# Routed experts of the first layer for three rows on scattered token blocks, the last row dense; constants of the key operands set earlier

## The reference, cut to what matters

```python
h = layernorm(x) * (1 + ca) + sa                # layer 0
x = x + ga * causal_attention_16_heads(h)       # 8 numbers a head, plus a shared rotary part of 32
h = layernorm(x) * (1 + cb) + sb
shared = gelu(h @ sW1 + sb1) @ sW2 + sb2        # one shared expert, 512 wide
w = softmax(h @ gW + gb)                        # 15 routed experts
topv, topi = top_k(w, 3)
gated = sum_over_k(one_hot(topi) * topv)
routed = sum_over_e(gated[e] * (gelu(h @ rW1[e] + rb1[e]) @ rW2[e] + rb2[e]))   # each 256 wide
x = x + gb * (shared + routed + h)
h = layernorm(x) * (1 + ca) + sa                # layer 1
x = x + ga * (attention_16_heads(h, no mask) @ w_proj + b_proj)
h = layernorm(x) * (1 + cb) + sb
x = x + gb * top_1_of_8_experts(h)              # relu, each 512 wide
```

## Time and profile before

| | |
|---|---|
| three runs, median (lowest to highest) | 937.01 us (936.86 to 939.99) |
| profiled execution: own time / span in the trace | 944.65 us / 942.9 us |
| mean granted clock of TensorE | 0.936 |
| TensorE products (PE) / weight loads (PEld) | 781.0 us, 83% / 492.7 us, 52% |
| VectorE (DVE) | 651.1 us, 69% |
| ScalarE (ACT) | 533.4 us, 57% |
| GpSimd (POOL) | 245.3 us, 26% |
| moved by DMA | 46.84 MB |

### The profile page before, as it was taken

How to read it: one execution, slowest core, us unless ns; L and a number is a source line. 1 busy time by engine, 2 the same in 40 slices (tenths; PEclk the granted TensorE clock), 3 DMA queues, 4 the chain that set the end, 5 groups by cost and what they waited for, 6 DMA issues and landing times. The chain is left out here.

```text
span 942.9 us, 12902 instructions
## 1 busy us (share of the span) xinstructions
PE 781.0 (83%) x4212; PEld 492.7 (52%) x4212; DVE 651.1 (69%) x1292; ACT 533.4 (57%) x976; POOL 245.3 (26%) x323
## 2 busy tenths in 40 slices
PE   4798888889987999999989789989989998338750
PEld 2454545445554677778767534444444443227740
DVE  5475586776672876866767696788988884438843
ACT  1345445546556677777767456656656666126740
POOL 3237655524421100000000230012212231144425
PEclk9589899999999999999999999999999999759985
DMA  5323411111100770000001121221321310021013
GB/s 167 68 62 90 85 25 31 36 36 35 27 10 1 224 223 0 1 1 1 1 12 22 31 62 34 43 72 24 83 43 37 89 25 13 0 74 45 29 37 87
DMA packets 56671, 46.84 MB, mean 50 GB/s; under 512 B 5831, under 2 KB 46620, under 8 KB 56604
## 3 DMA queue, kind: packets, MB, share of 16 engines
q1 hardware_dynamic: 55435, 43.72, 19.4%
q0 software_dynamic: 1024, 2.10, 0.8%
q10 hardware_dynamic: 144, 0.20, 0.1%
HBM read 14.67 MB, written 14.55 MB: 31 GB/s over the span
## 5 line engine op out<-in xcount | busy, mean ns | idle before, releaser
L923 ACT ACTIVATE ring<-single 128x512 f32<-128x512 f32 (+3 forms) x512 | 253.1, 518 | 196.8 <-PE single L1188 189.2
L1577 DVE TENSOR_REDUCE mneg<-pair 128x2 f32<-128x1024 f32 (+3 forms) x256 | 258.3, 1022 | 71.2 <-PE pair L1172 31.9
L1188 PE MATMUL single<-q_op,k_op 128*128 128x512 f32 (+3 forms) x512 | 215.7, 440 | 14.3 <-ACT ring L923 9.1
L1168 PE MATMUL pair<-k_op,q_op 128*128 128x512 f32 (+3 forms) x512 | 167.6, 406 | 13.0 <-DVE mneg L1577 11.4
L1188 PEld LDWEIGHTS single<-q_op,k_op 122*128 122x128 f32 (+1 forms) x512 | 96.8, 195 | 95.7 <-ACT ring L923 74.0
L1168 PEld LDWEIGHTS pair<-k_op,q_op 120*128 120x128 f32 (+1 forms) x512 | 98.2, 203 | 54.0 <-DVE mneg L1577 34.7
L1205 PE MATMUL p_o<-ring,vaug 128*9 128x512 f32 (+3 forms) x1024 | 114.0, 517 | 1.0 <-ACT ring L923 0.9
L1629 DVE TENSOR_TENSOR ring<-ring,single 128x1024 f32<-128x1024 f32 x60 | 73.2, 1221 | 46.9 <-ACT ring L952 45.4
L952 ACT ACTIVATE ring<-pair,cols 128x512 f32<-128x512 f32 x136 | 86.2, 686 | 32.5 <-PE pair L1252 26.7
L1634 DVE TENSOR_TENSOR hid_lo<-ring,hid_hi 128x1024 fp32r<-128x1024 f32 x68 | 83.3, 1224 | 22.9 <-ACT hid_hi L967 19.5
L967 ACT ACTIVATE hid_hi<-ring 128x1024 fp32r<-128x1024 f32 x68 | 72.2, 1062 | 31.3 <-issue 30.5
(11 more groups left out here) (311 smaller groups left out, 1347.7 us busy)
## 6 DMA issues: line engine op xcount, KB each, us to landing
xs<-zero SPq DMA_DIRECT2D x10, 1024.0 KB, 10.2
k_op<-hl SPq DMA_DIRECT2D x112, 64.0 KB
q_op<-hl SPq DMA_DIRECT2D x16, 256.0 KB
stage<-in_L_ffn_W_dram SPq DMA_DIRECT2D x8, 512.0 KB, 5.0
stage<-in_L_ffn_rW_dram SPq DMA_DIRECT2D x6, 512.0 KB, 4.9
q_op<-hl SPq DMA_DIRECT2D x48, 64.0 KB
xb<-xs SPq DMA_DIRECT2D x15, 128.0 KB, 2.0
xs<-yb SPq DMA_DIRECT2D x15, 128.0 KB, 1.7
```

The costliest lines, as they stand in the source:

```text
L923: exp_done.by(act.activation(ring[:, n % 8, lo:T], singles[n % 2][:, lo:T], ACT.Exp), (L, n))
L1168: ins = pe.matmul(both[:, i, 0:hi], r32(qs[:, P * qt:P * (qt + 1)]), r32(ks[:, 0:hi]), start=i == 0 or L == 1 or qt >= 2, stop=L == 1)
L1188: st_full.by(pe.matmul(singles[n % 2][:, lo:T], r32(ks[:, P * kc:P * (kc + 1)]), r32(qs[:, lo:T]), start=True, stop=True), (L, n))
L1577: s_taken.by(dve.tensor_reduce(mneg[:, G % 2, 2 * p:2 * p + 2, qt], both[:, :, 0:hi], axis=AX.X, op=ALU.max, negate=True), (L, m))
```

## The change

The key operands' constants are set in two memsets: those of the first eight heads right after the memset of `w_qkv`, those of the last four after the small memsets.

The routed experts of rows 0 to 2 are no longer dense. For each of these rows three parts are added beside the quads of the next row: `ht` transposes the high part of h back to rows of tokens, `rk` ranks each token's three choices within their experts and makes slots, and `bt` (once, after row 2) makes the table of blocks. GpSimd scatters each row's tokens with 12 indirect DMAs into a store cut into 13 x 1 MB, which SyncE cleared in rows 0 and 1 with transfers from the zeroed `w_qkv`. Between the attention and the dense stage stands a new loop, `routed_rows`, over 32 blocks (`NBLK0`) of 256 slots; its number is fixed by the sizes, not by where tokens go. Beside it stand the parts of the last row's output, norm and router (`BESIDE0`). The dense stage has 23 units left: the two shared ones for rows 0 to 2, all 17 for row 3. GpSimd gathers the results with 12 indirect DMAs a row, and `add_experts` (parts `c0`, `c1`, `c2`) weights them and adds them on VectorE. Weights of the second layer's attention are scaled in place, where copies were made before, and loads for the second layer go out in row 2.

```diff
+SPARSE = NB - 1
...
+NBLK0 = (TOP * T * SPARSE + E0 * (BLK - 1)) // BLK
+STORE = E0 * CAP0 + NBLK0 - TOP * T * SPARSE // BLK
+SLOTS = 8
...
-          (8, "b"): ["T.hin"], (8, "d"): ["T.lg"], (9, "b"): ["ot1"], (9, "d"): ["T.ex"], (10, "b"): ["mt3"],
...
+          (8, "b"): ["T.hin"], (8, "d"): ["T.lg"], (9, "b"): ["ot1", "T.ht"], (9, "d"): ["T.ex"], (10, "b"): ["mt3"],
+          (10, "d"): ["T.rt1"], (11, "b"): ["T.rt2"], (12, "b"): ["T.gt"], (12, "d"): ["T.rk"], (13, "b"): ["ot2"], (14, "b"): ["P.mt0"]},
...
+UNIT = [(r, u) for r in range(SPARSE) for u in (E0, E0 + 1)] + [(NB - 1, u) for u in range(UNITS)]
...
-DSTEPS = NB * UNITS + DEPTH + 3
...
...
+BESIDE = {7: ["c0"], 8: ["tb0"], 9: ["P.ns"], 10: ["P.na", "tb1"], 11: ["P.n1", "P.n2"], 12: ["P.n3", "P.ne"], 13: ["P.ln1"], 14: ["tb2"],
+          15: ["P.q"], 16: ["tb3"], 17: ["P.k", "c1"], 18: ["wo1"], 19: ["P.v"], 22: ["c2"]}
...
+            def clear(n):
+                first = 8 * BLK * n
+                sp.dma_start(xs[first:first + 8 * BLK, :].rearrange("(p b) d -> p b d", p=P),
+                             w_qkv[:, 0:D].unsqueeze(1).broadcast_to([P, 16, D])).then_inc(zeroed, 16)
...
             for r in range(NB):
                 G = NG * r
                 m_dma(0, G + 1)
                 head_dma(G + 3)
-                if r == 1:
+                if r == 0:
                     sp.wait_ge(pool_set, 1)
+                    apart(sp)
+                if r < 2:
+                    clear(6 * r)
+                    clear(6 * r + 1)
+                if r == 2:
...
+                if r < 2:
+                    clear(6 * r + 2)
+                    clear(6 * r + 3)
                 m_dma(0, G + 3)
+                if r == 2:
...
+                if r < 2:
+                    clear(6 * r + 4)
+                    clear(6 * r + 5)
...
+                    clear(12)
...
+            def block_out(n):
+                yb0_ready.wait_ge(sp, n)
+                at = sp.value_load(btab0[0:1, 0, n:n + 1], min_val=0, max_val=STORE - 1)
+                sp.dma_start(blocks_of[:, bass.ds(at, 1), :], yb0[:, n % 2, :, :].rearrange("p t d -> p (t d)").unsqueeze(1)).then_inc(yb0_out[n % 2], 16)
...
+            for n in range(SLOTS):
+                block_in(n)
+            for n in range(NBLK0):
+                block_out(n)
+                if n + SLOTS < NBLK0:
+                    block_in(n + SLOTS)
...
+            steps.step(pool.memset(k_op0[96:P, 0:2 * GH, :], 1.0))
...
-            pool.memset(k_op0[96:P, :, :], 1.0).then_inc(pool_set, 1)
...
+            pool.memset(k_op0[96:P, 2 * GH:3 * GH, :], 1.0).then_inc(pool_set, 1)
...
+                pool.indirect_dma_start(xs, bass.IndirectOffsetOnAxis(ap=idx0[:, s, t, k:k + 1], axis=0), h_tok0[:, t, :], None).then_inc(scattered0, 16)
...
+                    if r in (1, 2) and k >= 28:
+                        for i in range(2 * (k - 28), 2 * (k - 28) + 2):
+                            scatter0(r - 1, i)
+                    elif r in (2, 3) and k in (4, 5):
+                        for i in range(2 * k, 2 * k + 2):
+                            scatter0(r - 2, i)
+                    elif r == 3 and 22 <= k < 28:
+                        for i in range(2 * (k - 22), 2 * (k - 22) + 2):
+                            scatter0(r - 1, i)
...
+            for n in range(NBLK0):
+                e = pool.value_load(btab0[0:1, 1, n:n + 1], min_val=0, max_val=E0 - 1)
+                if n >= 3:
+                    y0_full.wait_ge(pool, n - 3)
+                    apart(pool)
+                pool.tensor_copy(b_blk0[:, n % 3, :].unsqueeze(1), b0_of[:, bass.ds(e, 1), :])
+                w0_here.by(pool.tensor_copy(r32(wst0[n % 3][:, :, :].unsqueeze(2)), w0_of[:, :, bass.ds(e, 1), :]), n)
...
+            def routed_rows():
+                def rounded_rows(n):
...
+                    xh0_ready.by(act.activation(r32(xt0_hi[:, n % 2, :]), singles[1][:, 0:BLK], ACT.Copy), n)
+                def hidden(n):
+                    e0_full.wait_ge(act, n)
+                    w0_here.wait_ge(act, n)
+                    if n >= 2:
+                        e0_lo.wait_ge(act, n - 2)
+                    apart(act)
+                    for c in range(2):
+                        ins = act.activation(hid0[:, n % 2, c, :], pairs[n % 2][:, 0, BLK * c:BLK * (c + 1)], ACT.Gelu, bias=b_blk0[:, n % 3, c:c + 1])
+                    gelu0_done.by(ins, n)
+                    gelu0_done.wait_ge(act, n)
+                    if n >= 2:
+                        y0_full.wait_ge(act, n - 2)
+                    apart(act)
+                    e0_hi.by(act.activation(r32(hid0_hi[:, n % 2, :, :]), hid0[:, n % 2, :, :], ACT.Copy), n)
+
...
+                for n in range(NBLK0 + 2):
+                    if n + 1 < NBLK0:
+                        rounded_rows(n + 1)
+                    if n < NBLK0:
+                        hidden(n)
+                    if n == 0:
+                        out_rows(0, 4 * NG - 1)
+                    if n >= 2:
+                        result(n - 2)
+                    for name, b in beside_block(n):
+                        part(name, b)
...
+            def routed_rows():
...
+                rows_in(0)
+                for n in range(NBLK0 + 2):
+                    if n + 1 < NBLK0:
+                        rows_in(n + 1)
+                    if n < NBLK0:
+                        first_layer(n)
+                    if 1 <= n <= NBLK0:
+                        second_layer(n - 1)
+                    if n >= 2:
+                        rows_out(n - 2)
+                    for name, b in beside_block(n):
...
+                        gelu0_done.wait_ge(pe, NBLK0 - 1)
+                        yb0_ready.wait_ge(pe, NBLK0 - 1)
...
+            def add_experts(r):
...
+                y = yg0[r]
+                dve.wait_ge(gathered0[r], 16 * TOP * NT)
...
+                apart(dve)
+                for t in range(NT):
+                    ins = dve.tensor_scalar(y[:, 0, t, :], y[:, 0, t, :], gate0[:, r, t, 0:1], None, ALU.mult)
...
+            def routed_rows():
...
+                    xl0_ready.by(dve.tensor_tensor(r32(xt0_lo[:, n % 2, :]), singles[1][:, 0:BLK], xt0_hi[:, n % 2, :], ALU.subtract), n)
...
+                    e0_lo.by(dve.tensor_tensor(r32(hid0_lo[:, n % 2, :, :]), hid0[:, n % 2, :, :], hid0_hi[:, n % 2, :, :], ALU.subtract), n)
...
+                    yt0_ready.by(dve.tensor_copy(yt0[:, n % 2, :], (p_o, p_m)[n % 2][:, 0:BLK]), n)
...
```

More of the change, by code:

```diff
@@ L33 @@
 C_SEL = C_RS + 64
[L34 removed]
+C_TAB = C_SEL + 16
 C_BASE = C_TAB + T
@@ L202, in every_part @@
                 out += beside_quad(a, q, "b") + beside_quad(a, q, "d")
-        out += [part for v in range(DSTEPS) for part in beside_unit(v)] if L == 0 else drain_parts()
+        if L == 0:
+            out += [part for n in range(NBLK0 + 2) for part in beside_block(n)]
+            out += [part for v in range(DSTEPS) for part in beside_unit(v)]
+        else:
+            out += drain_parts()
     return out
@@ L368, in build @@
         h_hi_ready, h_lo_ready = sig("h_hi_ready", order_of("hin")), sig("h_lo_ready", order_of("hin"))
-        units = list(range(NB * UNITS))
+        units = list(range(len(UNIT)))
         hid_full, gelu_done = sig("hid_full", units), sig("gelu_done", units)
-        routed = [v for v in units if v % UNITS < E0]
+        routed = [v for v in units if UNIT[v][1] < E0]
         spread, gated = sig("spread", routed), sig("gated", routed)
@@ L430, in tiles @@
             return ap.rearrange("p (t n) -> p t n", t=NT)
-        in_units = {part for v in range(DSTEPS) for part in beside_unit(v)}
+        in_units = {part for v in range(DSTEPS) for part in beside_unit(v)} | {part for n in range(NBLK0 + 2) for part in beside_block(n)}
+        last_p_m = [part for part in misc if part[1] < NB and part not in in_units][-1]
         first_bank = {("rp", 0): singles[0][:, :], ("q", 0): singles[1][:, :], ("rs", 0): pairs[0][:, 0, :], ("k", 0): pairs[1][:, 0, :]}
@@ L757, in _ @@
+            apart(pool)
+            gather0(0)
+            gather0(1)
             steps.step(pool.memset(hl1[:, 3, :], 0.0))
@@ L1566, in part @@
                     xn3_ready.by(norm_end("I", h_tok, xn3), key)
+            def add_experts(r):
+                y = yg0[r]
+                dve.wait_ge(gathered0[r], 16 * TOP * NT)
+                taken.wait_ge(dve, ("tb4", NB - 1))
+                apart(dve)
+                for t in range(NT):
+                    ins = dve.tensor_scalar(y[:, 0, t, :], y[:, 0, t, :], gate0[:, r, t, 0:1], None, ALU.mult)
+                step(ins)
+                for k in range(1, TOP):
+                    for t in range(NT):
+                        ins = dve.scalar_tensor_tensor(out=y[:, 0, t, :], in0=y[:, k, t, :], scalar=gate0[:, r, t, k:k + 1], in1=y[:, 0, t, :],
+                                                       op0=ALU.mult, op1=ALU.add)
+                    step(ins)
```

(2 more changed lines are left out.)

381 lines of the change are left out of this document (291 added, 90 removed), and 4 rows, old and new, of tables (LAST0, TABLE).

## The result

The changed kernel takes 955.3 us (median of four runs, 952.34 to 958.28) against 937.53 us before: 1.0177 times as long by the single runs, 95% interval 1.0137 to 1.0218. The forecast was 922, its range 902 to 947. The four executions fall in two pairs, 952.3 and 952.4 us at a mean granted clock of 0.905 to 0.907, and 958.2 and 958.3 us at 0.890; the profile is of the first pair.

The account below looks back on a forecast made before the run. TensorE was taken to bound the dense stage (busy 59.84 of 60 us) and nearly fill the attention. Terms -4.9 - 42.9 + 22 + 6 + 5 = -14.8 us took the median from 937.0 to 922, range 902 to 947.

Parts of the forecast that it names:

- 97.1 and 98.3 us forecast: Predicted lengths of the stretch of 32 expert blocks (97.1 us) and of the dense stage after it (98.3 us).
- 80.6 + 8: Block loop: 31 blocks at 2.6 us, 80.6, plus 8 us for the last row's transposes, normalisation and exponential.
- rival 2: Block loop: VectorE's subtraction of rounded hidden values, held by GpSimd's weight copies, makes blocks longer, kernel slower; chance 0.20.
- -42.9: Blocks and dense stage: 196.8 us where the stage took 239.7 before, a gain of 42.9 us.
- +33 us in the sum: Attention: its three added terms together, scatters 22, side work 6 and clears 5 us.
- The clears (+5): Attention, rows 0 and 1: clears on SyncE's queue delay maxima and head operands, +5 us (0 to 14).
- The side work (+6, 2 to 9): Attention: transposes, rank products, short VectorE operations and block table for three rows, 2 us a row, +6 us.
- The scatters (+22, 12 to 28): Attention: GpSimd's indirect DMAs between cuts delay TensorE's values, 7 us for each of two rows, 8 in row 3.
- Constants first (-4.9): Lead: with the key operands' constants memset split and moved, hT starts earlier, -4.9 us (at worst -3.5).

Follow-up runs that it names:

- e5: The changed kernel with its 13 clears issued by ScalarE, one every second quad, not on SyncE's queue: 946.71 us, ratio 1.0086.
- e12: The changed kernel without scatters, with 12 unread matmuls ahead of TensorE's row 3 wait and the clears issued by ScalarE: 920.99 us, ratio 0.9824.
- e1: The kernel before with only the memset of the key operands' constants split and moved: 936.26 us, ratio 0.9986.
- e10: The changed kernel without scatters, with 12 unread matmuls ahead of TensorE's 2.2 us wait in row 3: 926.69 us, ratio 0.9860.
- e11: The changed kernel with clears issued by ScalarE, scatters spread (none behind row 3's last cut) and 12 unread matmuls in row 3: 933.94 us, ratio 0.9958.
- e6: The changed kernel with the block table's operations replaced by two that write constants: 956.17 us, ratio 1.0198.
- e2: The changed kernel without the 36 indirect DMAs that scatter the rows and the waits for them: 935.82 us, ratio 0.9974.
- e7: The changed kernel without scatters, with constants for the block table and the rank part cut to two VectorE operations: 931.86 us, ratio 0.9927.
- e13: The changed kernel without scatters, with constants in place of ranks and table, and the clears issued by ScalarE: 915.39 us, ratio 0.9746.

## Why the prediction was wrong

**The stages that I priced best came out.** Blocks and dense stage: 97.1 and 98.3 us forecast, 101.4 (from the last cut) and 100.1 measured. From the first block's gelu (343.18) to the last one's (432.51) are 31 blocks with the last row's parts beside them, 89.3 us, 2.88 a block; I had 80.6 + 8. Two groups of the block loop in the changed kernel (count, busy, mean ns, idle before), and TensorE's waits from 343.2 to 432.5 (us in total, times, longest):

```profile
L1959 DVE TENSOR_TENSOR hid_lo<-hid,hid_hi 128x512 fp32r<-128x512 f32 x32 | 32.0, 1001 | 26.7 <-ACT hid_hi L1113 24.9
L1107 ACT ACTIVATE hid<-pair,b_blk 128x256 f32<-128x256 f32 x64 | 26.9, 474 | 6.6 <-PE pair L1458 5.5
...
PE p_m L1472 <- DVE hid_lo L1959: 8.4, 12, 2.0
PE p_o L1472 <- DVE hid_lo L1959: 5.3, 6, 2.0
```

VectorE's subtraction of hidden values takes 1.00 us in the mean, over the 0.42 to 0.66 that I counted and under the 1.2 of rival 2; TensorE (77.60) and ScalarE (74.55 of 101.4 us) are the fullest engines, VectorE has 64.23. Against -42.9 this term is -37.2 from last cut to last product. The Trainium skill (SBUF — State Buffer, section SBUF: two separate sides) has such subtractions and GpSimd's copies lock each other out; the trace agrees that they lengthen here (0.69 us where no copy of weights was under way as it began, up to 1.55 where one was). It was not free: TensorE waited 13.7 us in all for that subtraction. So rival 2's mechanism was at work, smaller than it said, and that the forecast of the stretch held beside it is in part luck.

**What failed is the price of the attention:** +33 us in the sum, +51.2 in the profile. Two of its three terms were too small, and the low clock behind TensorE's waits was in none of them. One by one:

**The clears (+5) were too small.** I looked for "four or five places where that passes its slack by 1 to 3 us". In row 0 alone they cost 8.6 us by e5 (69.5 to 60.9). Two waits of 2.94 and 3.60 us are 6.5 of them; the granted clock behind each (0.60 and 0.72 from 80 to 90 us, 0.50 from 110 to 115 in the changed kernel) goes with the rest. Out of the way, the clears give 8.6 us of the median back.

**The granted clock was not in the sum at all.** I priced every wait at its own length. A wait of TensorE can cost more than that: with the one of 2.22 us in row 3 filled, the median fell by 9.1 us (e10), 5.5 of them to be seen in row 3. The rows of before showed it, 0.93 in the first of the earlier trace rows against 1.00, and the prediction does not speak of it.

**The side work (+6, 2 to 9) was too small:** 14 to 17 us by e12, of which 4 to 6 or more are ranks and table. My count took the operations' durations; I did not follow who waits for them. TensorE's transpose of the attention's outputs waits 2.07 us for VectorE to write the slots `idx` of the rank part (at 176.41 and again at 253.39), and everything behind it in TensorE's list waits too.

**The scatters (+22, 12 to 28) held in size:** 19.5 us. The steps were 2.85 us as forecast. But the size is in part luck: row 2 lost 6 us beside a wait that I had not seen (3.78 us, to 203.16), and whether some of the 19.5 is clock and not GpSimd's time is not shown (the clock of row 3 is 0.81 with the scatters and 0.82 without).

**Constants first (-4.9) was right in the profile and wrong in the median:** hT started at 13.96, but e1 gained 1.6 us, not clear of noise. One of three profiles with the memset in its old place has no such wait. I made the sum against one execution, which had it, and carried that over to the median.

In medians: 922.0, and 3.3 for the lead, 3.6 for the clears (8.6 by e5 for 5), 11 for side work, 5.7 for blocks and dense, 1.7 for the rest, less 2.5 for the scatters, are 944.8. The remaining 10 us are about what e10 gave for the clock in row 3, but no run shows that they are the same: where causes overlap such terms do not strictly add, and with the scatters in place the matmuls gave no clear gain (e11). Rival 2 (944 to 950, slower) had the right side by luck: it put the loss into the blocks, at over 3.1 us each, and they took 2.88.

## What to carry to other kernels

A profile is one execution: before a saving is counted, look whether the two events that collide do so by chance (here GpSimd began at 11.87 us or at 12.74, when a load had landed), and how far runs spread. When something is added to a nearly full TensorE stage, give each new idle stretch a price for itself and a range for the clock behind it: waits of 1.87 to 3.60 us were followed here by anything from none to 41 us of half clock, the same 2.22 us wait by 41 in e6, by 34 in e2 and by 7 in e7 and e13. A few matmuls ahead of the wait may be worth more than shortening it. Large transfers belong in a queue that carries nothing that an engine waits for: with the same clears in another engine's queue row 0 lost 0.6 us in place of 9.2.

## What the runs showed of the hardware

Twelve matmuls whose result nobody reads made a program of 936 us 9.1 us faster (e10 against e2). Transfers of 1 MB and the loads between them kept 8 KB of maxima, issued behind them on the same queue, from landing for about 3 us, while with the clears in another queue row 0 had no such wait at a higher traffic (197 GB/s in e12, 160 in the changed kernel). VectorE operations on four numbers a partition took 1.10 to 1.33 us beside a copy on GpSimd of 1.03 us, and 0.16 without. Leaving out 13 VectorE operations of the block table changed nothing that could be measured (956.17 for 955.3 us).
